# A graph-attention and mixture-of-experts layer on one Trainium2 core: raw tokens in the setup, adjacency in column halves, and another order of the units of a head pair

## The chip, the core and the metric

The kernel runs on one core of a Trainium2 chip. The metric is device time in microseconds (us) of one launch. A core has TensorE (PE, matrix multiplications into PSUM), VectorE (DVE), ScalarE (ACT), GpSimd (POOL) and SyncE (SP, which here only issues DMA transfers). Each engine takes its instructions in the order in which they are written, and a semaphore wait holds everything behind it on that engine.

## What is computed

The layer is graph attention, followed by a mixture of experts that the change doesn't touch:

```python
# N = 2048 tokens, D = 512, H = 16 heads of 32
xn = layernorm(x)                                  # no weights
seq = (xn @ W_seq).reshape(N, H, DH)
s = leaky_relu(score1[:, :, None] + score2[:, None, :], 0.2)   # seq . a1, seq . a2
s = s + (1.0 - adj)[None] * -65500.0
attn = softmax(s, axis=-1)
hidden = einsum('hij,jhd->ihd', attn, seq).reshape(N, D) @ W_out + b_out
x = x + elu(hidden)
x = x + moe_ffn(layernorm(x))
```

## The kernel before

**Units.** The exponential of a leaky ReLU of a sum splits into products of row and column factors, with one of two factor pairs on either side of a threshold. So a head needs, for half of the output rows (IC = 1024), a 0/1 mask of 16 tiles of 128 neighbours by 1024 rows, and matrix products of the mask and of the adjacency with the values. One such product is a unit: 8 row tiles (i), each with 16 matmuls on the mask (L798) and 16 on the adjacency (L802). There are 32 units, four to a pair of heads; the index k in 0..3 of a pair p says head k // 2 and column half k % 2. Masks have MB = 4 buffers, values vs have two (one for each head), sums two.

**The work for a unit.** compare: VectorE compares 6 of the 16 tiles (L653) and ScalarE the other 10 (L600, a steep sigmoid), both against a score row broadcast to all partitions (s1b), which SP loads again (L558) as soon as both have compared. mask_own (L661) and mask_acts (L668) put the adjacency onto VectorE's and ScalarE's tiles; m_ready counts the latter. products (POOL, L742 and L744) scales the values of a head, split_high (ACT, L608) and low_values (DVE, L682) split them into two fp16 parts. TensorE runs the unit when m_ready and sums_ready say so, and lo_ready for a head's first unit. collect (DVE, L675) takes the sums out of PSUM. A unit waits for the collection of the unit two before it. combine (POOL, L752 and L757) scales and adds them into hid. VectorE's loop step (p, k) is: collect(p, k), compare(p + 1, k), low_values if k is odd, mask_own(p + 1, k), mask_acts of the k before.

**The setup.** x is loaded in 4 groups (L185), W_seq on ScalarE's queue (L196), then the constants. VectorE takes mean and variance (stats, L280), GpSimd the inverse root, VectorE normalises x in place (norm, L291). TensorE transposes a tile of x (L429) into PSUM; ScalarE rounds it to a high part (L204), VectorE takes the rest as the low part (low_x, L298). project (L438) is 12 matmuls for a token tile, scores (L449) 12 for four tiles. W_seq is transposed too (L409) for the columns of the scores (L418). Scores go back to token order (L486) and to DRAM as rows (s1_rows). The adjacency comes in 16 loads of 1 MB with three buffers (L193), VectorE turns each into fp8 (L305), TensorE adds up the neighbours of each column (degrees, L460, 64 matmuls), and where there are none VectorE sets all (apply_empty_rows, L395 and L397).

The order is the hand-written order of calls on each engine. The loops of ScalarE, VectorE and GpSimd over the pairs are hardware loops, TensorE's is unrolled.

## Time and profile before

| what | value |
|---|---|
| median of 3 runs | 1078.7 us (1076.36 to 1081.2) |
| the profiled execution itself | 1076.02 us |
| its span, first to last instruction | 1074.2 us |
| TensorE, VectorE, ScalarE, GpSimd busy | 95%, 75%, 60%, 23% of the span |
| granted TensorE clock, mean | 0.981 of full |
| setup, to the first unit | 0 to 129.8 us |
| the 32 units | 129.8 to 505.3 us |
| projection and experts | 505.3 to 1074.2 us |

"Busy" is the time in which an engine had an instruction running. A share over the whole span mixes stages; the setup and the units are to be read apart. In the granted clock 1.00 stands for 2.4 GHz and 0.50 for 1.2 GHz. Names such as arena stand for one large block of SBUF, in which most tiles lie, so a group is best known by its line.

### The profile page before, as it was taken

What the parts mean: (1) busy time and instruction counts of PE and PEld (TensorE: products, weight loads), DVE (VectorE), ACT (ScalarE), POOL (GpSimd) and SP (SyncE); (2) the same over time, 40 slices, a digit from 0 to 9 for tenths busy, and PEclk for the clock granted to TensorE, in tenths of its full rate; (3) what the DMA queues carried; (4) which work ended last, traced back from release to release, by engine and by line L of the source; (5) the groups of instructions that cost most, each with busy time, mean ns of one, the idle gap of its engine ahead of it and who ended that gap; (6) DMA issues with size and microseconds to landing.
All of it is one profiled execution on the core that took longest, in us unless ns stands there. A gap on an engine that the chain in (4) does not pass through costs nothing.

```text
span 1074.2 us, 27252 instructions
## 1 busy us (share of the span) xinstructions
PE 1018.5 (95%) x11304; PEld 894.5 (83%) x11304; DVE 806.5 (75%) x1200; ACT 648.9 (60%) x971; POOL 247.7 (23%) x271
## 2 busy tenths in 40 slices
PE   4799499999999999998999999999999999999998
PEld 4577299999999999998677888888888878878887
DVE  4746999999999999993599633347686569976554
ACT  3226499999999999960456433344345546655441
POOL 1100223333443333344342000000065000006500
PEclk8899699999999999999899999999999999999999
DMA  8357011111111111260834200020044124454242
GB/s 316 118 175 281 20 38 46 42 61 42 62 41 56 47 42 56 83 219 4 298 118 148 108 1 1 1 79 1 1 157 167 59 79 120 132 159 122 79 138 98
DMA packets 51458, 102.45 MB, mean 95 GB/s; under 512 B 5889, under 2 KB 25985, under 8 KB 48770
## 3 DMA queue, kind: packets, MB, share of 16 engines
q1 hardware_dynamic: 44386, 81.68, 22.4%
q10 hardware_dynamic: 3888, 10.72, 2.9%
q0 software_dynamic: 3072, 8.39, 2.4%
q8 instruction: 91, 1.49, 0.6%
q14 instruction: 21, 0.17, 0.0%
HBM read 74.69 MB, written 26.08 MB: 94 GB/s over the span
## 4 chain that ended last, share of the span: by engine, by line
PE 47%; DVE 2%; issue 2%; DMA 1%; POOL 0%; ACT 0%; SPq 0%; POOLq 0%; DVEq 0%; ACTq 0%
PE bank L1177 16%; PE bank L1644 16%; PE bank L1009 3%; PE bank L1721 2%; PE bank L1672 1%; PE bank L1673 1%; PE bank L1675 1%; DMA xs<-sorted_latent_rows 1%; PE bank L1691 1%; PE bank L1665 1%; PE bank L1629 1%; PE bank L1006 1%; PE bank L1627 1%; PE bank L997 1%; PE bank L1018 1%
## 5 line engine op out<-in xcount | busy, mean ns | idle before, releaser
L600 ACT ACTIVATE arena<-arena 128x1024 fp8e4<-128x1024 f32 x320 | 336.4, 1135 | 3.0 <-ACT arena L592 3.0
L798 PE MATMUL bank<-arena 128*128 128x132 f16 x4096 | 283.8, 221 | 15.6 <-DVE arena L682 15.0
L798 PEld LDWEIGHTS bank<-arena 128*128 128x128 fp8e4 x4096 | 245.0, 97 | 17.7 <-DVE arena L682 15.5
L1177 PE MATMUL bank<-xt,up_parts 128*128 128x512 f32 x768 | 186.2, 391 | 0.0
L1644 PE MATMUL bank<-down_parts,h_parts 128*128 128x512 f32 x768 | 184.5, 389 | 0.0
L802 PE MATMUL bank<-arena 128*128 128x66 f16 x4096 | 172.6, 195 | 1.6 <-issue 1.6
L1644 PEld LDWEIGHTS bank<-down_parts,h_parts 128*128 128x128 f32 x768 | 143.9, 188 | 30.2 <-issue 0.2
L653 DVE TENSOR_SCALAR arena<-arena 128x1024 uint8<-128x1024 f32 x192 | 166.4, 933 | 0.0
L1177 PEld LDWEIGHTS bank<-xt,up_parts 128*128 128x128 f32 x768 | 142.3, 188 | 28.7 <-ACT relu_sb L1126 0.2
L802 PEld LDWEIGHTS bank<-arena 128*128 128x128 fp8e4 x4096 | 153.7, 98 | 1.9 <-issue 1.9
L1151 DVE TENSOR_TENSOR relu_sb<-relu_sb 128x512 f32<-128x512 f32 x64 | 44.3, 692 | 117.9 <-ACT relu_sb L1126 117.2
L1126 ACT ACTIVATE relu_sb<-bank 128x512 f32<-128x512 f32 x64 | 38.3, 598 | 148.3 <-PE bank L1177 139.0
L752 POOL TENSOR_TENSOR arena<-arena 128x264 f32<-128x264 f32 x64 | 45.4, 731 | 218.9 <-DVE arena L668 195.9
L668 DVE TENSOR_TENSOR arena<-arena 128x2560 uint32<-128x2560 uint32 x32 | 90.8, 2838 | 0.2
L1145 ACT CAST down_parts<-down_sb 128x512 fp32r<-128x512 f32 x64 | 39.8, 622 | 72.6 <-PE bank L1644 62.9
L1598 POOL DMA_INDIRECT sorted_latent_rows<-latent,slot_idx x32 | 34.7, 1085 | 209.0 <-DVE slot_idx L1464 191.0
L1166 DVE TENSOR_TENSOR down_parts<-down_sb,down_parts 128x512 fp32r<-128x512 f32 x64 | 44.2, 691 | 50.2 <-ACT down_parts L1145 47.4
...
L742 POOL TENSOR_TENSOR arena<-arena 128x512 f32 (+1 forms) x32 | 48.6, 1520 | 63.2 <-ACT arena L209 25.1
L661 DVE TENSOR_TENSOR arena<-arena 128x1536 uint32<-128x1536 uint32 x32 | 56.1, 1753 | 0.6
L675 DVE TENSOR_REDUCE arena<-bank 128x198 f32<-128x396 f32 (+1 forms) x96 | 44.1, 513 | 15.0 <-PE bank L798 15.0
L1009 PE MATMUL bank<-wo_parts,hT 128*128 128x512 f32 x192 | 49.7, 409 | 0.0
...
## 6 DMA issues: line engine op xcount, KB each, us to landing
hid<-in_adjT SPq DMA_DIRECT2D x16, 1024.0 KB, 5.2
arena<-s_rows SPq DMA_DIRECT2D x30, 512.0 KB, 3.7
...
arena<-in_x SPq DMA_DIRECT2D x4, 1024.0 KB, 12.0
...
```

What stands on the lines that cost most here:

```text
L600: last = nc.scalar.activation(m8[:, k, j, :], s1b[:, k % 2, :], ACT.Sigmoid, bias=bias_now[:, k // 2, j:j + 1], scale=STEEP, saturate=False)
L653: last = nc.vector.tensor_scalar(mu8[:, k, j, :], s1b[:, k % 2, :], neg_s2[:, 2 * p + k // 2, j:j + 1], float(ONE8), ALU.is_gt, ALU.mult)
L661: nc.vector.tensor_tensor(mw[:, k, 0:DVE_J, :], mw[:, k, 0:DVE_J, :], adjw[:, 0:DVE_J, cols], ALU.bitwise_and).then_inc(own_masked, 1)
L668: nc.vector.tensor_tensor(mw[:, k, DVE_J:, :], mw[:, k, DVE_J:, :], adjw[:, DVE_J:, cols], ALU.bitwise_and).then_inc(m_ready, 1)
L742: nc.gpsimd.tensor_tensor(vtmp[:, :, c * W1:c * W1 + DH], vh, val[:, :, bass.ds(h, 1)].to_broadcast([P, T, DH]), ALU.mult)
L752: last = nc.gpsimd.tensor_tensor(scaled[:, k % 2, :, c * W1:(c + 1) * W1], sums[:, k % 2, :, c * W1:(c + 1) * W1], coef[:, h, tiles, c:c + ...
L798: last = nc.tensor.matmul(o, m8[:, k, j, i * P:(i + 1) * P], vs[:, b, j, :], start=(j == 0), stop=(j == T - 1))
L802: nc.tensor.matmul(od, adj8[:, ja, (k % 2) * IC + i * P:(k % 2) * IC + (i + 1) * P], vs[:, b, ja, :].rearrange("p (s c) -> p s c", s=2)[:, ...
L1009: last = nc.tensor.matmul(bank[2 + t % 2][:, :], hT[:, t % 2, a, k, :], wo_parts[:, b, k, :], start=False, stop=(n == len(terms) - 1))
L1151: nc.vector.tensor_tensor(r, r, r, ALU.mult).then_inc(sq_ready, 1)
L1177: last = nc.tensor.matmul(bank[6 + s % 2][:, :], sa[:, s % 2, a, k, :], xt[c][:, b, k, :], start=(i == 0), stop=(i == len(mm) - 1))
L1644: last = nc.tensor.matmul(ob[t][:, :], hhl[:, s % 2, a, t * P:(t + 1) * P], sb_[:, s % 2, b, :], start=(n == 0 and (a, b) == TERMS[0]), st ...
```

## The change

W_seq comes transposed, and first on SP's queue. VectorE takes the mean of each of its columns away (centre_w), so that raw tokens can be multiplied by it; x is no longer normalised, and ScalarE multiplies the inverse root in when it copies the projected values out of PSUM (copy_v). Projections use two PSUM banks in turn instead of four. Scores take 8 matmuls instead of 12, with 64 rows out, and their two halves are added after the way back to token order (natural_scores); a second set of 16 transposes makes the rows for DRAM.

The adjacency comes in 32 loads of half a tile row: first the first column half of all 16 tiles, then the second, with five buffers and no wait for x. VectorE casts the even ones, ScalarE the odd ones. Which columns have no neighbour is found from an OR of the 16 tiles (any_neighbour, on VectorE) and 8 matmuls for each half. The second half's come between the first and the second unit.

In a pair, k now says column half k // 2 and head k % 2. The loop body of VectorE has low_values ahead of compare, at k = 2 and 3, and the first collection stands ahead of compare(0, 3).

```diff
-AB = 3
+AB = 5
+HALVES = 2 * T
...
+        SEQ_BANK = [bank[2], bank[3]]
+        WA_BANK = bank[3]
+        ST_BANK = [bank[4], bank[7]]
+        ROW_BANK = [bank[4], bank[7], bank[5], bank[6]]
+        DEG_BANK = [bank[6], bank[7]]
+
+        def cast_source(q):
+            return adj_in[:, q % AB, :], adj8[:, q % T, (q // T) * IC:(q // T + 1) * IC]
...
+            sp.dma_start(wt_sb, w_seqT.rearrange("(c p) k -> p c k", p=P)).then_inc(wt_loaded, 16)
             for g in range(4):
                 sp.dma_start(x_sb[:, 4 * g:4 * g + 4, :],
                              x[512 * g:512 * g + 512, :].rearrange("(t p) d -> p t d", p=P)
                              ).then_inc(x_loaded[g], 16)
-            for g in range(4):
-                sp.wait_ge(x_loaded[g], 16)
-            for n in range(T):
-                if n >= AB:
-                    sp.wait_ge(adj_cast, n - AB + 1)
-                sp.dma_start(adj_in[:, n % AB, :], adjT[n * P:(n + 1) * P, :]).then_inc(adj_loaded[n % AB], 16)
+            for q in range(HALVES):
+                if q >= AB:
+                    sp.wait_ge(cast_by_act if (q - AB) % 2 else cast_by_dve, (q - AB) // 2 + 1)
+                sp.dma_start(adj_in[:, q % AB, :], adjT[(q % T) * P:(q % T + 1) * P, (q // T) * IC:(q // T + 1) * IC]
+                             ).then_inc(adj_loaded[q % AB], 16)
...
-                    nc.scalar.copy(v_sb[:, t, :], SEQ_BANK[t % 4][:, :]).then_inc(v_copied, 1)
+                    act.wait_ge(std_ready, t // 4 + 1)
+                    nc.scalar.activation(v_sb[:, t, :], SEQ_BANK[t % 2][:, :], ACT.Copy,
+                                         scale=rstd[:, t:t + 1]).then_inc(v_copied, 1)
...
+            def cast(*odd):
+                for q in odd:
+                    act.wait_ge(adj_loaded[q % AB], 16 * (q // AB + 1))
+                    src, dst = cast_source(q)
+                    nc.scalar.activation(dst, src, ACT.Copy, scale=-1.0, saturate=False).then_inc(cast_by_act, 1)
...
+            for s in range(8):
+                copy_v(s)
+                if s < 7:
+                    high_x(2 * s + 2, 2 * s + 3)
+                if s % 2:
+                    copy_scores(s // 2)
+                if s >= 2:
+                    cast(2 * s - 3)
+            cast(13)
+            copy_v(8)
+            cast(15)
+            copy_v(9)
+            cast(17)
+            copy_v(10)
+            cast(19)
...
+            def centre_w():
+
+                dve.wait_ge(wt_loaded, 16)
+                for c in range(KD):
+                    last = nc.vector.bn_stats(w_stat6[:, c, :], wt_sb[:, c, :])
+                step(last)
+                for c in range(KD):
+                    last = nc.vector.bn_aggr(w_mv[:, c, :], w_stat6[:, c, :])
+                step(last)
+                for c in range(KD):
+                    last = nc.vector.tensor_scalar(wt_sb[:, c, :], wt_sb[:, c, :], w_mv[:, c, 0:1], None, ALU.subtract)
+                last.then_inc(w_centred, 1)
...
-            def norm(g):
-                dve.wait_ge(std_ready, g + 1)
-                for t in range(4 * g, 4 * g + 4):
-                    nc.vector.tensor_scalar(x_sb[:, t, :], x_sb[:, t, :], mv[:, t, 0:1], rstd[:, t:t + 1],
-                                            ALU.subtract, ALU.mult).then_inc(xn_ready, 1)
...
+            def cast(*even):
+
+                for q in even:
+                    dve.wait_ge(adj_loaded[q % AB], 16 * (q // AB + 1))
+                    src, dst = cast_source(q)
+                    nc.vector.tensor_scalar(dst, src, -1.0, None, ALU.mult, saturate=False).then_inc(cast_by_dve, 1)
...
+            def any_neighbour(half):
+
+                words = slice(half * IC // 4, (half + 1) * IC // 4)
+
+                def cast_up_to(tiles):
+                    dve.wait_ge(cast_by_dve, (T * half + tiles) // 2)
+                    dve.wait_ge(cast_by_act, (T * half + tiles) // 2)
+
+                cast_up_to(8)
+                step(nc.vector.tensor_tensor(anyw, adjw[:, 0:4, words], adjw[:, 4:8, words], ALU.bitwise_or))
+                cast_up_to(12)
+                step(nc.vector.tensor_tensor(anyw, anyw, adjw[:, 8:12, words], ALU.bitwise_or))
+                cast_up_to(16)
+                nc.vector.tensor_tensor(anyw, anyw, adjw[:, 12:16, words], ALU.bitwise_or).then_inc(any_ready, 1)
...
+            def scores_to_tokens():
+                pe.wait_ge(st_copied, 4)
+                for t in range(T):
+                    last = nc.tensor.transpose(bank[5 + t // 8][:, (t % 8) * 4 * H:(t % 8 + 1) * 4 * H],
+                                               sT[:, t * P:(t + 1) * P], ident[0:4 * H, 0:4 * H])
+                last.then_inc(s_in_psum, 1)
+
+            for s in range(8):
+                project(s)
+                if s < 7:
+                    transpose(2 * s + 2, 2 * s + 3)
+                if s % 2:
+                    scores(s // 2)
+            project(8)
+            scores_to_tokens()
+            project(9, 10)
+            scores_to_rows()
+            project(11)
+            degrees(0)
+            project(12, 13, 14, 15)
...
-                    b = k // 2
-                    if k % 2 == 0:
+                    b = k % 2
+                    if k < 2:
+                        act.wait_ge(act_compared, 4 * p + k - 1)
...
-                compare_rows(0, DVE_J, 10)
-                copy_v(10)
-                compare_rows(0, 10, 12)
-                copy_v(11)
-                compare_rows(0, 12, 14)
-                copy_v(12)
-                compare_rows(0, 14, T)
-                copy_v(13, 14, 15)
+                compare_rows(0, DVE_J, DVE_J + 2)
+                copy_v(14)
+                cast(27)
+                compare_rows(0, DVE_J + 2, DVE_J + 4)
+                copy_v(15)
+                cast(29)
+                compare_rows(0, DVE_J + 4, DVE_J + 6)
                 split_high(0, 0)
+                compare_rows(0, DVE_J + 6, T)
+                cast(31)
+                nc.scalar.copy(bias_now[:, 1, :], step_bias[:, 1, :]).then_inc(bias_copied, 1)
+                act.wait_ge(bias_copied, 2)
                 act.wait_ge(s1_staged[1], 16)
-                compare_rows(1, DVE_J, T)
+                compare_rows(1, DVE_J, DVE_J + 4)
                 split_high(0, 1)
+                compare_rows(1, DVE_J + 4, T)
...
+                def body(p, last=False, first=False):
                     for k in range(4):
                         if last and k == 3:
                             split_low()
-                        dve.wait_ge(unit_in_psum, 4 * p + k + 1)
-                        collect(p, k)
+                        if k or not first:
+                            dve.wait_ge(unit_in_psum, 4 * p + k + 1)
+                            collect(p, k)
                         if not last:
+                            if k >= 2:
+                                low_values(p + 1, k % 2)
                             compare(p + 1, k)
-                            if k % 2:
-                                low_values(p + 1, k // 2)
                             mask_own(p + 1, k)
 
                         if k == 0:
@@ -707,29 +778,32 @@
...
-                scale_columns()
-                cast_adjacency(10)
                 dve.wait_ge(seq_in_psum, 8)
                 compare(0, 0)
-                cast_adjacency(11, 12, 13, 14, 15)
-                apply_empty_rows((0, 1))
+                cast(24, 26)
                 mask_own(0, 0)
+                cast(28)
+                low_values(0, 0)
                 mask_acts(0, 0)
-                apply_empty_rows((2, 3))
+                cast(30)
                 dve.wait_ge(seq_in_psum, T)
                 compare(0, 1)
-                low_values(0, 0)
                 mask_own(0, 1)
+                any_neighbour(1)
+                low_values(0, 1)
                 mask_acts(0, 1)
-                low_values(0, 1)
+                apply_empty_rows((2, 3))
                 compare(0, 2)
                 mask_own(0, 2)
+                mask_acts(0, 2)
+                dve.wait_ge(unit_in_psum, 1)
+                collect(0, 0)
                 compare(0, 3)
                 mask_own(0, 3)
-                mask_acts(0, 2)
-                with dve.Fori(0, PAIRS - 1) as p:
-                    body(p, False)
-                body(PAIRS - 1, True)
+                body(0, first=True)
+                with dve.Fori(1, PAIRS - 1) as p:
+                    body(p)
+                body(PAIRS - 1, last=True)
...
-                        b = k // 2
-                        if k % 2 == 0:
+                        b = k % 2
+                        if p == 0 and k == 1:
+                            degrees(1)
+                        if k < 2:
                             pe.wait_ge(lo_ready, 2 * p + b + 1)
```

Three places of the order of instructions follow. The first is the start of VectorE's queue. Before, the constants and then x are waited for:

```order
L309 MEMSET score_columns 128x352
L312 TENSOR_SCALAR arena<-arena 128x4x16 [waits consts_loaded]
L312 TENSOR_SCALAR arena<-arena 128x4x16
L280 BN_STATS arena<-arena 128x6 [waits x_loaded0]
L280 BN_STATS arena<-arena 128x6 x3
```

Now the same start, with the weights in front:

```order
L348 MEMSET score_columns 128x512
L351 TENSOR_SCALAR arena<-arena 128x4x16 [waits consts_loaded]
L351 TENSOR_SCALAR arena<-arena 128x4x16
L306 BN_STATS arena<-arena 128x6 [waits wt_loaded]
L306 BN_STATS arena<-arena 128x6 x3
L309 BN_AGGR arena<-arena 128x2 [waits dve_step]
L309 BN_AGGR arena<-arena 128x2 x3
L312 TENSOR_SCALAR arena<-arena 128x512 [waits dve_step]
L312 TENSOR_SCALAR arena<-arena 128x512 x3
```

Nine instructions on the weights' columns moved ahead of the statistics of x, and TensorE's first instruction waits for them.

The second place is VectorE between the mask of the first unit and the first collection. Before, from mask_acts(0, 0) on (L395 and L397 are the empty columns, L653 a comparison, L661 and L668 the masks, L682 low_values):

```order
L395 TENSOR_SCALAR arena<-bank 128x512
L397 TENSOR_TENSOR arena<-arena 128x16x128
L653 TENSOR_SCALAR arena<-arena 128x1024 x6
L682 TENSOR_TENSOR arena<-arena 128x16x66
L661 TENSOR_TENSOR arena<-arena 128x1536
L668 TENSOR_TENSOR arena<-arena 128x2560
L682 TENSOR_TENSOR arena<-arena 128x16x66
L653 TENSOR_SCALAR arena<-arena 128x1024 x6
L661 TENSOR_TENSOR arena<-arena 128x1536
L653 TENSOR_SCALAR arena<-arena 128x1024 x6
L661 TENSOR_TENSOR arena<-arena 128x1536
L668 TENSOR_TENSOR arena<-arena 128x2560
```

Now, from the comparison for the second unit (L723) on, with any_neighbour at L409 to L413, low_values at L752 and the collection at L745:

```order
L731 TENSOR_TENSOR arena<-arena 128x1536 [waits dve_compared]
L409 TENSOR_TENSOR hid<-arena 128x1024 [waits cast_by_act,cast_by_dve]
L411 TENSOR_TENSOR hid<-hid,arena 128x1024 [waits cast_by_act,cast_by_dve,dve_step]
L413 TENSOR_TENSOR hid<-hid,arena 128x1024 [waits cast_by_act,cast_by_dve,dve_step]
L752 TENSOR_TENSOR arena<-arena 128x16x66 [waits hi_copied]
L738 TENSOR_TENSOR arena<-arena 128x2560 [waits own_masked,act_compared]
L420 TENSOR_SCALAR arena<-bank 128x512 [waits deg_in_psum]
L422 TENSOR_TENSOR arena<-arena 128x16x128 [waits dve_step]
L420 TENSOR_SCALAR arena<-bank 128x512 [waits deg_in_psum,dve_step]
L422 TENSOR_TENSOR arena<-arena 128x16x128 [waits dve_step]
L723 TENSOR_SCALAR arena<-arena 128x1024 [waits s1_staged_lo,dve_step]
```

The OR, the second half's empty columns and one wait for TensorE stand there now between the second unit's comparison and the third's.

The third place is a step with k odd in the loop on VectorE. Before:

```order
L675 TENSOR_REDUCE arena<-bank 128x132
L653 TENSOR_SCALAR arena<-arena 128x1024 [waits s1_staged_hi]
L653 TENSOR_SCALAR arena<-arena 128x1024 x5
L681 REGISTER_ALU
L682 TENSOR_TENSOR arena<-arena 128x16x66 [waits hi_copied]
L660 REGISTER_ALU
L661 TENSOR_TENSOR arena<-arena 128x1536 [waits dve_compared]
L668 TENSOR_TENSOR arena<-arena 128x2560 [waits own_masked,act_compared]
```

Now, the step with k = 3:

```order
L745 TENSOR_REDUCE arena<-bank 128x198 x2
L745 TENSOR_REDUCE arena<-bank 128x132
L752 TENSOR_TENSOR arena<-arena 128x16x66
L723 TENSOR_SCALAR arena<-arena 128x1024 x6
L731 TENSOR_TENSOR arena<-arena 128x1536
L738 TENSOR_TENSOR arena<-arena 128x2560
```

low_values moved from behind the comparison to the place right behind the collection.

## Rows read from the trace of the kernel before

**Rows 1.** Stretches: engines busy and count, TensorE clock, DMA share, GB/s; loop of units.
```profile
164.80:480.90 316.10, 313.92 (x6933) 311.99 (x6931) 314.56 (x312) 302.15 (x302) 114.61 (x135) 1.00 0.20 67
```

**Rows 2.** VectorE in order of time, one pair of loop steps: start us, us, instruction.
```profile
350.86 1.38 DVE L675 TENSOR_REDUCE arena<-bank 128x198 f32<-128x396 f32 x3
352.15 4.62 DVE L653 TENSOR_SCALAR arena<-arena 128x1024 uint8<-128x1024 f32 x6
356.70 1.25 DVE L682 TENSOR_TENSOR arena<-arena 128x1056 f16<-128x1056 f32 x1
357.87 1.75 DVE L661 TENSOR_TENSOR arena<-arena 128x1536 uint32<-128x1536 uint32 x1
359.53 2.81 DVE L668 TENSOR_TENSOR arena<-arena 128x2560 uint32<-128x2560 uint32 x1
...
363.57 6.09 DVE L653 TENSOR_SCALAR arena<-arena 128x1024 uint8<-128x1024 f32 x6
...
374.11 1.38 DVE L675 TENSOR_REDUCE arena<-bank 128x198 f32<-128x396 f32 x3
```

**Rows 3.** TensorE in order of time, two tiles of one unit.
```profile
345.39 1.09 PE L798 MATMUL bank<-arena 128*128 128x132 f16 x16
...
346.83 1.09 PE L798 MATMUL bank<-arena 128*128 128x132 f16 x16
```

**Rows 4.** Who waited for whom, 128 to 500 us: us in total, times, longest.
```profile
PEld bank L798 <- DVE arena L675: 2.2, 9, 0.3
```

**Rows 5.** VectorE in order of time, setup, and the second collection of the loop.
```profile
12.68 2.46 DVE L280 BATCH_NORM_STATS2 arena<-arena 128x6 f32<-128x512 f32 x4
...
20.88 1.91 DVE L291 TENSOR_SCALAR arena<-arena 128x512 f32<-128x512 f32 x4
...
88.05 4.06 DVE L653 TENSOR_SCALAR arena<-arena 128x1024 uint8<-128x1024 f32 x6
...
108.46 2.29 DVE L397 TENSOR_TENSOR arena<-arena 128x2048 uint32<-128x2048 uint32 x1
...
163.52 1.38 DVE L675 TENSOR_REDUCE arena<-bank 128x198 f32<-128x396 f32 x3
```

**Rows 6.** TensorE in order of time, the setup up to the first unit.
```profile
12.37 3.54 PE L409 MATMUL bank<-arena,hid 128*128 128x128 f32 x16 [12.37 <-DMA arena<-in_a_mask]
16.68 4.85 PE L418 MATMUL bank<-arena 128*128 128x32 f32 x32 [0.77 <-ACT arena L215]
...
25.68 0.78 PE L438 MATMUL bank<-w_high,x_high 128*128 128x512 f32 x1
...
30.18 0.39 PE L438 MATMUL bank<-w_high,x_high 128*128 128x512 f32 x1
...
57.69 1.03 PE L429 MATMUL bank<-arena 128*128 128x128 f32 x8
...
78.85 0.50 PE L438 MATMUL bank<-w_high,x_high 128*128 128x512 f32 x1
...
95.33 4.49 PE L460 MATMUL bank<-arena 128*128 128x512 fp8e4 x20
...
129.83 0.29 PE L798 MATMUL bank<-arena 128*128 128x132 f16 x1 [15.01 <-DVE arena L682]
```

**Rows 7.** A stretch as in rows 1, in which adjacency loads land.
```profile
20.00:26.50 6.50, 5.86 (x26) 5.17 (x26) 4.84 (x8) 2.46 (x5) 1.92 (x1) 0.50 1.00 423
```

**Rows 8.** DMA issues by line: KB each, median us to landing.
```profile
hid<-in_adjT SPq DMA_DIRECT2D x16, 1024.0 KB, 5.2
arena<-s_rows SPq DMA_DIRECT2D x30, 512.0 KB, 3.7
```

**Rows 9.** ScalarE in order of time, first comparisons.
```profile
87.31 4.27 ACT L600 ACTIVATE arena<-arena 128x1024 fp8e4<-128x1024 f32 x4
```

**Rows 10.** GpSimd in order of time, same stretch as rows 2.
```profile
364.78 1.52 POOL L742 TENSOR_TENSOR arena<-arena 128x512 f32 x1
...
374.40 1.24 POOL L752 TENSOR_TENSOR arena<-arena 128x264 f32<-128x264 f32 x2 [5.33 <-DVE arena L668]
```

322 lines of the change are left out of this document (153 added, 169 removed).

## The prediction, made before the changed kernel ran

> **What bounds the kernel now.** I read the stretches first, then the engines in order of time, and stage by stage, since the mean over the span hides that two stages have different limits. In the 32 units TensorE looks like the limit, but between 164.8 and 480.9 us VectorE is busy for 314.6 of 316.1 us, with no gap to give away [rows 1]. A pair of its loop steps takes 23.25 us, from 350.86 to 374.11 [rows 2]. A tile of a unit takes 1.44 us on TensorE [rows 3], so two units of eight tiles take 23.04. The two are within 1%, VectorE is the slower one, and TensorE waits a little for its collections, nine times by this view [rows 4]. So it matters little when the first unit starts; what counts is the time at which VectorE ends collect(0, 1) and with it frees the fourth unit. I call that time W. It is 164.8 now: 163.52 and three reductions [rows 5]. From W to the end of the last unit, 505.3, it is 340.5 us, and from there to the end of the span 568.9, which the change doesn't touch. In the setup nothing is saturated: TensorE starts at 12.4, waits for the low parts of x, and stands still for 15.0 us ahead of the first unit at 129.83, with VectorE's queue in front of it [rows 6].
>
> **The start.** VectorE must now centre the weights before TensorE does anything: 2.46 us of statistics as for four x tiles, four passes of 512 columns like the norms, 1.91, and 0.5 for small ones [rows 5], 4.9 in all. In return the 1 MB of weights and the constants are no longer behind 2 to 3 MB of other loads. With 423 GB/s [rows 7] that megabyte takes 2.5 us after the first bytes; I take 6.2 us for the end of this wait, which puts the first matmul at 11.3. The bound above is that the constants land at 12.3 as before [rows 6]; this costs 6 at the start and, as statistics then run while TensorE works, 4 at W.
>
> **Projections.** On TensorE then follow the transposes of W 3.5, two of x at half clock 1.9, the score columns 4.85 and one projection 4.5 (25.68 to 30.18), so 26.2 [rows 6]. Up to the scores in token order: 8 projections at 2.75 (six from 78.85 to 95.33), 14 tiles transposed at 0.5 (eight instructions in 1.03, four to a tile), 32 score matmuls at 0.23 instead of 48, and 1.4 for the way to tokens [rows 6]: 22.0 + 7.2 + 7.4 + 1.4 = 38, so 64.2, where it is 78.9 now. This holds if TensorE never waits. For each projection step of 4.65 us ScalarE has a copy of values, two high parts, a cast and half a score copy, about 3.0; VectorE has 1.9, and 4.9 in the three steps with statistics. The two PSUM banks cover that: a projection waits for the copy two before. The norms (16 passes, 7.7 us of VectorE) and their wait for GpSimd are gone; what is late next is the low part of x, with 1 to 3 us to spare.
>
> **To the first unit.** Two projections and the transposes into rows end at 71.5. Four small copies, the transfer to DRAM and the one back, 3.7 each [rows 8], exponentials, one copy and one cast put the score rows into SBUF at 82.5. The adjacency does not hold this up: with five half loads in flight at 1.3 us each (0.52 MB at 423 GB/s) the sixteenth half is cast at 64.5. From 83.6 on ScalarE's own queue is the path: a table load 1.3, ten comparisons at 1.05 [rows 9], two value copies 1.1, casts 27 and 29 at 1.05 each, the split 1.0, waits 0.4, which gives 100.0; with mask_acts, 2.8 [rows 2], the first unit starts at 102.8. TensorE ends its projections at 87.0 and stands still for 16, as now.
>
> **From the first unit to W**, all on VectorE: cast 0.6, comparison 4.0 [rows 5], own mask 1.7, the OR 3.4 (three times 1024 words, where 1536 take 1.75), low values 1.2, mask 2.8 [rows 2]: 116.5. It waits for the 8 degree matmuls behind the first unit (11.5 us, and an estimated 3.3 for a start at half clock, where everything takes twice as long) until 118.6; behind this wait stand the third and fourth masks. Then 6.1 for two column blocks of empty columns (2.29 and the flags [rows 5]), 4.0, 1.7, 2.8 and a collection 1.3: the third unit at 134.5, TensorE having waited 3. Then 4.5, 1.7, 5.5, 1.7, 2.8, 1.3, and W is 151.9. The same sum over the old order of calls gives 163.1 where the row says 164.8; I add that 1.7, so W = 153.6, 11.2 earlier. The first unit gains 25 of which 14 are lost again, because the second half's casts, OR and empty columns moved from ahead of it to behind it.
>
> **From W to the end.** The work in a loop step is the same. What shifts is the company of VectorE's comparison. With GpSimd's products beside it (from 364.78) it takes 6.09, with a combine (from 374.40) about 4.6 [rows 2, 10], alone 4.06 [rows 5]. At k = 2 and 3 the combine now falls beside the collection and low_values, and I estimate 0.35 + 0.45 saved in four steps, 5.6 over seven passes. TensorE's own pace limits this: 29 units at 11.52 are 334.1, 1.6 for gaps in its instruction stream, and 1.4 as the sixth unit now waits for low_values: W + 337.1. If nothing is saved it is W + 340.5. I take 338. In the trace the split (a wait of VectorE for ScalarE would be new, as low_values moved forward by 4.6) is done 4 us ahead of VectorE's step, so I cost this at nothing; if that lead were gone, 1 to 2 us a time.
>
> The combine beside two-input operations is where the Trainium skill speaks against me. The row shows a comparison slowed in the company of GpSimd [rows 2, 10]. By the Trainium skill (SBUF — State Buffer, Who interferes with whom) a VectorE instruction with two SBUF inputs contends with a GpSimd one that reads SBUF, and one of the two blocks fully, while a reduction never does. By that rule only the part beside the collection is saved, and the sum would be nearer to W + 340.
>
> **The sum.** 505.3 becomes 153.6 + 338 = 491.6, which is 13.7 less. The profiled execution took 1076.0 (span 1074.2 and 1.8 around it), so 1062.3 for its like; it stands 2.7 under the median of 1078.7. On the median: **1065.0**.
>
> **Rivals.** (A) VectorE remains the limit and nothing is saved by the shift: W + 341.7 with the low_values wait, 495.3, a gain of 10: 1068.7. For it: VectorE's 99.5% [rows 1]. Together with late constants (4) it is 1072.7. (B) The first unit decides, as TensorE's 95% would have it: 25.3 gained, 1053.4. Against it: the same row, and TensorE's waits for collections [rows 1, 4]. (C) The early gain isn't there at all, because ScalarE, with 16 casts more, holds the projections: then the scores are in token order near 75, not 64, and W falls by 0 to 3: 1076 to 1079. Against it: 3.0 of 4.65 us a step. (D) Slower: half loads land no faster than whole ones. A load now lands in 5.2 us, and a half-size one from DRAM in 3.7, not 2.6 [rows 8], so some of the time doesn't shrink. With 2.7 us a half the path above waits for loads 15 to 31, W is 168.7 and the end 506.7 to 510.4 (1080 to 1084); with 3.0 W is 175.5, the end 513.5 to 517.2, and the kernel takes 1087 to 1090. It loses from 2.5 us a half on, and measurably from 2.8. Against it: 423 GB/s with only three loads in flight [rows 7].
>
> The Trainium skill sides with D in part: DMA: Bandwidth & Descriptors, Rules for kernel authors, wants transfers of at least 1 MiB for full bandwidth, and these are half of that. The row shows 423 GB/s for whole ones and nothing for halves.
>
> **How the numbers follow.** The forecast (gain 11 to 17) 0.55, A with or without late constants 0.2, B 0.03, C 0.12, D 0.06, the rest 0.04. What a measurement of this kernel can tell from no change is about 0.5%, 5.4 us. Faster by more than that holds the forecast, B and most of A: 0.78; within it C and a little of A: 0.15; slower D and the rest: 0.07. The range: below, W 151.9 and TensorE's pace give 489.0, a gain of 16.3, and runs go 2.3 under their median, 1059; above, C's better end, 1076.
>
> **What would show it.** Right: first matmul near 11, scores in token order near 66, first unit near 104 with ScalarE the last one waited for, a gap of about 3 us on TensorE ahead of the third and again the fourth unit, collect(0, 1) ending near 154, and comparisons at k = 2 and 3 shorter than 6.1 and 4.6. Wrong: VectorE waiting for loads in the setup, TensorE waiting for x's low parts by more than 3 us in total, VectorE waiting for hi_copied in the loop, or W to the end over 342.

## The result and the profile after

The changed kernel takes 1065.5 us (median of 4 runs, 1063.7 to 1066.7), the kernel before 1078.2 beside it: a ratio of 0.987, 95% interval 0.986 to 0.989. That is faster by 1.3%, small but with the whole interval below 1, and 0.5 us from the forecast.

The profiled execution took 1063.7 us. I read it by marks. T is the start of the transposes that bring the scores into token order (their end stands in this table, as in the prediction), U the start of the first unit, W the end of the second collection, L the start of the last collection, which is the end of the last unit.

| | before | predicted | after |
|---|---|---|---|
| scores in token order (end) | 78.9 | 64.2 | 63.0 |
| U | 129.8 | 102.8 | 104.2 |
| W | 164.8 | 153.6 | 150.5 |
| L | 505.3 | 491.6 | 491.5 |
| W to L | 340.5 | 338.0 | 341.0 |
| L to the end of the span | 568.9 | 568.9 | 570.4 |

TensorE in order of time (start us, us, instruction, idle before and what ended it); these answer [rows 6]:

```profile
13.71 3.65 PE L468 MATMUL bank<-arena 128*128 128x128 f32 x16 [13.71 <-DVE arena L312]
...
26.45 1.03 PE L487 MATMUL bank<-arena 128*128 128x128 f32 x8
...
53.57 1.03 PE L487 MATMUL bank<-arena 128*128 128x128 f32 x8
...
61.80 1.21 PE L517 MATMUL bank<-arena 64*128 64x64 f32 x16
...
104.17 0.27 PE L874 MATMUL bank<-arena 128*128 128x132 f16 x1 [18.33 <-DVE arena L738]
...
134.24 0.29 PE L874 MATMUL bank<-arena 128*128 128x132 f16 x1 [3.90 <-DVE arena L745]
...
150.63 0.23 PE L874 MATMUL bank<-arena 128*128 128x132 f16 x1 [3.16 <-DVE arena L745]
```

The first matmul waits for the centred weights (L312) until 13.7, later than before. From there to T it never stands: three double steps of projections take 9.04 us each. Then it stands 18.3 us for the first mask, 3.9 for the first collection and 3.2 for the second.

VectorE over the same time, answering [rows 5]:

```profile
8.65 0.42 DVE L351 TENSOR_SCALAR arena<-arena 128x64 f32<-128x64 f32 x2 [7.25 <-DMA arena<-in_a_mask]
...
62.13 0.69 DVE L345 TENSOR_SCALAR arena<-hid 128x1024 fp8e4<-128x1024 f32 x1 [4.67 <-DMA hid<-in_adjT]
...
97.03 1.26 DVE L752 TENSOR_TENSOR arena<-arena 128x1056 f16<-128x1056 f32 x1 [7.42 <-ACT arena L673]
101.20 2.82 DVE L738 TENSOR_TENSOR arena<-arena 128x2560 uint32<-128x2560 uint32 x1 [2.91 <-ACT arena L665]
...
140.69 4.06 DVE L723 TENSOR_SCALAR arena<-arena 128x1024 uint8<-128x1024 f32 x6
...
149.19 1.38 DVE L745 TENSOR_REDUCE arena<-bank 128x198 f32<-128x396 f32 x3
```

ScalarE is the last one waited for ahead of the first unit, twice, 7.4 us for the split (L673) and 2.9 for the comparisons (L665). From 101.2 to W VectorE has no wait left.

The loop, VectorE, then GpSimd beside it, answering [rows 2, 10]:

```profile
347.07 1.38 DVE L745 TENSOR_REDUCE arena<-bank 128x198 f32<-128x396 f32 x3
348.37 1.34 DVE L752 TENSOR_TENSOR arena<-arena 128x1056 f16<-128x1056 f32 x1
349.64 6.08 DVE L723 TENSOR_SCALAR arena<-arena 128x1024 uint8<-128x1024 f32 x6
...
361.46 1.32 DVE L752 TENSOR_TENSOR arena<-arena 128x1056 f16<-128x1056 f32 x1
362.71 4.45 DVE L723 TENSOR_SCALAR arena<-arena 128x1024 uint8<-128x1024 f32 x6
...
372.90 6.30 DVE L723 TENSOR_SCALAR arena<-arena 128x1024 uint8<-128x1024 f32 x6
...
384.94 4.63 DVE L723 TENSOR_SCALAR arena<-arena 128x1024 uint8<-128x1024 f32 x6
...
394.02 1.38 DVE L745 TENSOR_REDUCE arena<-bank 128x198 f32<-128x396 f32 x3
```

```profile
360.43 1.24 POOL L826 TENSOR_TENSOR arena<-arena 128x264 f32<-128x264 f32 x2 [5.96 <-DVE arena L738]
361.85 1.44 POOL L831 TENSOR_TENSOR hid<-arena 128x264 f32 x1 [0.18 <-POOL arena L826]
...
385.50 0.87 POOL L831 TENSOR_TENSOR hid<-arena 128x264 f32 x1 [0.19 <-POOL arena L826]
```

Four steps take 46.95 us, from 347.07 to 394.02; two pairs of steps as in [rows 2] took 46.56 (350.86 to 397.42). The comparisons are as long as before. The last addition of a combine takes 1.44 us beside low_values (361.85) where it takes 0.87 beside a comparison (385.50). These two rows also show how long the addition stays beside the comparison: it ends 0.6 us into the one at k = 3 and 1.4 us into the one at k = 1.

The stretch of the loop, answering [rows 1], who TensorE waited for, answering [rows 4], and the loads, answering [rows 8]:

```profile
150.49:466.66 316.17, 312.04 (x6878) 311.03 (x6879) 315.25 (x309) 292.65 (x292) 122.43 (x135) 0.99 0.19 66
```

```profile
PE bank L874 <- DVE arena L752: 3.3, 5, 0.7
```

```profile
hid<-in_adjT SPq DMA_DIRECT2D x32, 512.0 KB, 5.7
arena<-s_rows ACTq DMA_DIRECT2D x2, 512.0 KB, 4.7
```

VectorE is busy for 315.3 of 316.2 us. A half load lands in 5.7 us with up to five in flight. From 66 to 72 us, where the DMA engines were busy throughout, they moved 371, 416 and 395 GB/s in stretches of 2 us, which is 1.3 to 1.4 us a half, as the prediction had it. ScalarE still waits for a load at a costly place, right ahead of the table load and the comparisons of mask 0:

```profile
84.29 1.06 ACT L224 ACTIVATE arena<-hid 128x1024 fp8e4<-128x1024 f32 x1 [3.15 <-DMA hid<-in_adjT]
```

The table load then starts at 85.36.

### The profile page after: what moved, and what is told of

It is laid out like the page before. It is cut to its first block, busy times and chain, and to the rows that moved or that the text cites. A ratio compares the mean times of both kernels' runs of the same rounds, so it can differ in the third digit from the quotient of the medians.

```text
span 1061.9 us, 27192 instructions
## 1 busy us (share of the span) xinstructions
PE 1003.7 (95%) x11256; PEld 889.3 (84%) x11256; DVE 801.6 (75%) x1197; ACT 666.4 (63%) x990; POOL 247.5 (23%) x271
## 4 chain that ended last, share of the span: by engine, by line
PE 48%; issue 2%; DVE 2%; DMA 1%; POOL 0%; ACT 0%; SPq 0%; POOLq 0%; DVEq 0%; ACTq 0%
PE bank L1253 16%; PE bank L1720 16%; PE bank L1085 3%; PE bank L1797 2%; PE bank L1748 1%; PE bank L1749 1%; PE bank L1751 1%; DMA xs<-sorted_latent_rows 1%; PE bank L1767 1%; PE bank L1705 1%; PE bank L1741 1%; PE bank L1082 1%; PE bank L1703 1%; PE bank L1073 1%; PE bank L1094 1%
## 5 line engine op out<-in xcount | busy, mean ns | idle before, releaser
L665 ACT ACTIVATE arena<-arena 128x1024 fp8e4<-128x1024 f32 x320 | 336.4, 1135 | 2.5 <-ACT arena L657 1.4
L874 PE MATMUL bank<-arena 128*128 128x132 f16 x4096 | 285.1, 221 | 29.4 <-DVE arena L738 18.3
L723 DVE TENSOR_SCALAR arena<-arena 128x1024 uint8<-128x1024 f32 x192 | 166.2, 932 | 0.0
L878 PEld LDWEIGHTS bank<-arena 128*128 128x128 fp8e4 x4096 | 154.3, 98 | 0.1
L1686 POOL DMA_INDIRECT y_gathered<-sorted_expert_rows,slot_idx x32 | 32.6, 1018 | 153.6 <-DMA sorted_expert_rows<-expert_y 132.8
L745 DVE TENSOR_REDUCE arena<-bank 128x198 f32<-128x396 f32 (+1 forms) x96 | 44.2, 516 | 14.2 <-PE bank L874 14.2
## 6 DMA issues: line engine op xcount, KB each, us to landing
sorted_latent_rows<-zeros SPq DMA_DIRECT2D x1, 4992.0 KB, 18.3
```

The source lines that it names most:

```text
L665: last = nc.scalar.activation(m8[:, k, j, :], s1b[:, k % 2, :], ACT.Sigmoid, bias=bias_now[:, k % 2, j:j + 1], scale=STEEP, saturate=False)
L723: last = nc.vector.tensor_scalar(mu8[:, k, j, :], s1b[:, k % 2, :], neg_s2[:, 2 * p + k % 2, j:j + 1], float(ONE8), ALU.is_gt, ALU.mult)
L745: last = nc.vector.reduce_sum(sums[:, k % 2, t0:t0 + n, :], bank[3 * (k % 2) + g][:, 0:n * WV].rearrange("p (t s c) -> p t c s", t=n, s=2) ...
L874: last = nc.tensor.matmul(o, m8[:, k, j, i * P:(i + 1) * P], vs[:, b, j, :], start=(j == 0), stop=(j == T - 1))
L878: nc.tensor.matmul(od, adj8[:, ja, (k // 2) * IC + i * P:(k // 2) * IC + (i + 1) * P], vs[:, b, ja, :].rearrange("p (s c) -> p s c", s=2)[ ...
```

## What the runs were to settle

Theory T: all of VectorE's work from the first unit to W, and its pace in the loop, set the end; when the first unit starts does not. Rival R1: the first unit, or TensorE's pace after it, decides. (The letters of theories and rivals have nothing to do with the marks T, U, W and L.) Three more questions came from the terms that missed: why nothing was saved in the loop, what ScalarE's queue is worth, and which part of the change brought the gain at W.

Single executions of one kernel differ by up to 12 us ("norms back": 1067.7 to 1079.9), so I read the marks in each trace beside the medians. A trace is of one execution, so a mark of one trace carries that execution's scatter. The change itself was run once more beside three of the later kernels.

> The changed kernel itself, unchanged, on the chip of the next three kernels, so that differences of two or three microseconds can be read against it. Every theory: 1065.5 us, and in the trace W (the end of the second collection) 46.3 us behind the first unit's start and the end of the last unit 341.0 us behind W.

The table holds all the kernels. In the eight traces whose loop is untouched W to L is 341.0 to 341.4, so a difference of one microsecond there can be read.

| kernel | T | U | W | W to L | L to end | median | ratio to before |
|---|---|---|---|---|---|---|---|
| the change | 61.8 | 104.2 | 150.5 | 341.0 | 570.4 | 1065.5 | 0.987 (0.986 to 0.989) |
| the change again | 63.8 | 107.9 | 154.3 | 341.1 | 571.0 | 1066.7 | 0.987 (0.984 to 0.989) |
| 5 us more on VectorE | 59.7 | 101.5 | 153.8 | 341.1 | 570.8 | 1073.9 | 0.995 (0.993 to 0.997) |
| late first unit | 62.8 | 119.8 | 152.2 | 341.1 | 578.3 | 1065.8 | 0.987 (0.985 to 0.989) |
| low parts behind | 62.1 | 105.2 | 152.9 | 342.7 | 572.2 | 1069.9 | 0.991 (0.988 to 0.994) |
| last casts on VectorE | 62.5 | 104.9 | 151.7 | 341.2 | 573.6 | 1065.4 | 0.985 (0.982 to 0.988) |
| values first | 59.6 | 100.2 | 147.8 | 341.0 | 571.8 | 1065.1 | 0.986 (0.983 to 0.988) |
| low parts mixed | 62.4 | 103.1 | 150.4 | 341.9 | 571.0 | 1065.1 | 0.985 (0.982 to 0.987) |
| no multiplications on GpSimd | 62.6 | 105.9 | 153.7 | 336.0 | 570.5 | 1060.8 | 0.982 (0.979 to 0.984) |
| a row to ScalarE | 63.3 | 106.1 | 152.9 | 338.4 | 573.2 | 1063.1 | 0.985 (0.983 to 0.988) |
| norms back | 69.4 | 111.2 | 157.8 | 341.4 | 572.2 | 1073.2 | 0.995 (0.992 to 0.997) |
| quarter loads | 62.8 | 107.7 | 154.8 | 341.3 | 569.5 | 1066.3 | 0.990 (0.987 to 0.993) |
| score rows before loads | 60.1 | 100.7 | 147.5 | 338.6 | 572.5 | 1061.0 | 0.983 (0.982 to 0.985) |

Read it by the columns. Leaving out "norms back", T still goes from 59.6 to 63.8, and L to the end from 569.5 to 578.3. The second is scatter in the mixture of experts that nothing here touches. The first goes with TensorE's granted clock in the first projection, as the last section shows.

## Does the first unit decide?

**Five microseconds more on VectorE**, ahead of the comparison of mask 3:

```
 collect(0, 0)
+for _ in range(3):
+    words of mw[:, 3, 0:6] = adjw & adjw; wait for them
 compare(0, 3)
```

> Three needless operations of 1.68 us each on VectorE (words of the adjacency joined with themselves into the mask buffer that the next comparison overwrites, each waited for before the next) stand between the collection of the first unit and the comparison of mask 3: 5.0 us plus three short drains, 5.2 us in all. The result is untouched. Theory T (the stretch up to the second collection and the unit loop are VectorE's, so that all of VectorE's work ahead of the loop is on the path): +5.2 us against the changed kernel, 1070.7. Rival R1 (the start of the first unit decides, and TensorE's pace after it): nothing before the fourth unit is touched, TensorE pays at most what exceeds its own slack there, +0 to +1.5 us, 1065.5 to 1067.

**Late first unit:**

```
-if p == 0 and k == 1:
-    degrees(1)
+if p == 0 and k == 0:
+    degrees(1)
+    pe.wait_ge(m_ready, 2)
```

> TensorE is made to wait with the first unit until the mask of the second is ready too, and counts the neighbours of the second column half before it instead of behind it. The first unit then starts near 118.0 instead of 104.2, 13.8 us later; no work is added. Theory T: VectorE never waits for a unit there (it comes to the first collection at 132.8 and to the second at 149.2, the units would end near 130.8 and 142.4), so W, the end of the second collection, stays at 150.5 and the time at 1065.5, +0 to +1 us. Rival R1 (the first unit decides): TensorE's three waits ahead of the second to the fourth unit, 1.3, 3.9 and 3.2 us, can take up 8 of the 13.8 us, the rest is paid: +5.5 us or more, 1071.

TensorE and VectorE of the second kernel in order of time:

```profile
115.99 3.35 PE L535 MATMUL bank<-hid,arena 128*128 128x512 fp8e4 x8 [29.10 <-DVE hid L413]
119.80 0.23 PE L875 MATMUL bank<-arena 128*128 128x132 f16 x1 [0.47 <-DVE arena L738]
```

```profile
150.86 1.38 DVE L745 TENSOR_REDUCE arena<-bank 128x198 f32<-128x396 f32 x3
```

The first unit starts at 119.8, T + 57.0 instead of T + 42.4, and VectorE still waits for nothing: W is T + 89.3 against T + 88.7 and T + 90.5 in the two traces of the change. The median is 1065.8. A first unit that stands 12.9 to 14.6 us further behind T costs nothing that can be measured; R1 falls. In the first kernel U to W grows from 46.3 to 52.3 us, 6.0 for 5.2 added, and W to L stays at 341.1, so that added work is paid in full. Its median rose by more, 7 to 8 us, from times that scatter over 10 us: 5.2 us on the ratio of the change would be 0.992, just below the interval. What the trace doesn't hold of that I leave open.

## The low parts and the company of GpSimd

**Low parts behind the comparison again:**

```
-if k >= 2:
-    low_values(p + 1, k % 2)
 compare(p + 1, k)
+if k >= 2:
+    low_values(p + 1, k % 2)
 mask_own(p + 1, k)
```

> In the unit loop the low parts of the values are taken behind the comparison again (steps k = 2 and 3), instead of between collection and comparison. Theory T has two halves. In the loop, the semaphore that VectorE waits for between comparison and own mask is hidden again behind the low parts: 46.95 us in four steps go back to about 46.55, 7 times 0.4 is 2.8 us less. At the end, the last pair's second unit waits for its low values, which come a comparison (4.5 us) and a drain later, and three units of 11.5 us follow them: +5.6 us. Net +2.8 us, 1068.3. Rival R2 (the loop's pace alone decides, the tail is covered): -2.8 us, 1062.7. Rival R3 (the combination's company beside the comparison costs VectorE what the prediction charged, 0.8 us in four steps): +5.6 from the loop, +8 or more with the tail, 1073.

```profile
168.81 0.29 PE L874 MATMUL bank<-arena 128*128 128x132 f16 x1 [4.04 <-DVE arena L752]
```

```profile
440.28 1.38 DVE L745 TENSOR_REDUCE arena<-bank 128x198 f32<-128x396 f32 x3
...
459.10 1.69 DVE L752 TENSOR_TENSOR arena<-arena 128x1056 f16<-128x1056 f32 x1
...
495.61 1.39 DVE L745 TENSOR_REDUCE arena<-bank 128x198 f32<-128x396 f32 x3 [6.31 <-PE bank L874]
```

From the second collection to the 27th (149.19 to 440.96 in the change, 151.64 to 440.28 here) VectorE needs 288.6 us instead of 291.8: 3.1 less, where 2.8 were expected. The end takes back 4.8, where 5.6 were expected, and W to L is 1.7 longer. R2 and R3 fall by W to L; the median, 1069.9, is 1.6 us above the forecast and its times go from 1063.7 to 1075.0. But TensorE also waits 4.0 us once for low parts, after the fourth unit, and then hardly again. That led to the next kernel.

**Low parts mixed**, behind for the first six pairs, ahead for the last, on top of "values first" below:

```
-with dve.Fori(1, PAIRS - 1) as p:
+with dve.Fori(1, PAIRS - 2) as p:      # low parts behind
     body(p)
+body(PAIRS - 2, ahead=True)
```

> As the kernel before it, and in the unit loop the low parts of the values come behind the comparison for the first six pairs and ahead of it only for the last, where the tail waits for them. Theory T: the run with the low parts behind everywhere took four steps in 46.56 us for 46.95 and lost 4.1 us at the end; this keeps the first, 6 times 0.4 is 2.4 us, and not the second: 1058.1, W to end 338.6. Rival R2' (the gain in the loop was bought by the later end, VectorE being held by TensorE's chain): W to end stays at 341.0, 1060.5.

W to L is 341.9. The saving of VectorE is there and the last low parts come in time, yet nothing is gained: R2' holds. TensorE stands 4.0 us for low parts at 166.25 and from there to 492.3 needs 326.1 us for 28 units, of which 322.6 is its own pace. The change loses the same 4 us in five waits of 0.5 to 0.7 us and 0.7 in its instruction stream, the other order in one piece. From there on TensorE is nearly at its own pace, so VectorE's saving has nothing left to shorten.

**No multiplications on GpSimd:**

```
-scaled = sums * coef        # two instructions
-hid = scaled[0:W1] + scaled[W1:]
+hid = sums[0:W1] + sums[W1:]
```

> GpSimd's two multiplications in the combination of every unit are left out (it only adds the two halves of the sums, so the output is not the reference's); GpSimd then works 1.24 us less beside each step of VectorE. Theory P (GpSimd's company costs VectorE in proportion to how long it lasts, about 0.45 us for each microsecond beside a comparison): the comparisons of steps 1 and 3 fall from 4.63 and 4.45 us to about 4.1, those of 0 and 2 by 0.4 to 0.5 us each, four steps take 45.2 us of VectorE's work, so that TensorE's 46.08 us become the pace: W to end 341.0 - 7.3 times 0.87, about 334.7, time 1059. Rival Q (a comparison pays a lump for being near GpSimd's work, whatever its length, or pays for the products alone): less than 0.5 us in four steps, W to end 338 or more, time 1062.5 to 1065.5.

VectorE in order of time:

```profile
340.83 1.38 DVE L745 TENSOR_REDUCE arena<-bank 128x198 f32<-128x396 f32 x3
...
343.29 5.71 DVE L723 TENSOR_SCALAR arena<-arena 128x1024 uint8<-128x1024 f32 x6
...
355.91 4.07 DVE L723 TENSOR_SCALAR arena<-arena 128x1024 uint8<-128x1024 f32 x6
...
365.72 5.54 DVE L723 TENSOR_SCALAR arena<-arena 128x1024 uint8<-128x1024 f32 x6
...
377.00 4.06 DVE L723 TENSOR_SCALAR arena<-arena 128x1024 uint8<-128x1024 f32 x6
...
385.51 1.38 DVE L745 TENSOR_REDUCE arena<-bank 128x198 f32<-128x396 f32 x3
```

The comparisons without GpSimd beside them fall to 4.07 and 4.06, as long as alone, and the other two by 0.4 and 0.8. Four steps take 44.68 us and TensorE is the pace: W to L 336.0. Q's numbers are out (it wanted W to L 338 or more), and P's are the nearer ones (334.7). But P's reason, a price in proportion to time, is not shown. In this kernel the addition ends before the comparisons of k = 1 and 3 start, so they have no company left; and in the change 0.6 us of an addition beside a comparison cost 0.39 us (4.45 for 4.06) where 1.4 us of a combine cost 0.57. 336.0 is also the measured end of TensorE's own pace: the prediction's lower bound was W + 337.1.

**A row to ScalarE.** The same gain with the work done: on top of "values first", ScalarE takes one comparison more in step k = 0 of every pair but the first.

```
+def rows_of(p, k): return 5 if k == 0 and p != 0 else 6
-for j in range(DVE_J):                   # VectorE
+for j in range(rows_of(p, k)):
-compare_rows(k, DVE_J, T)                # ScalarE
+compare_rows(k, rows_of(p, k), T)
```

> The kernel with the values first and, in the unit loop, one of VectorE's six comparisons of step k = 0 on ScalarE (five rows of 16 left on VectorE in that step, six in the others). Theory B (in the loop VectorE's 46.95 us for four steps are the pace and TensorE's 46.08 only just below it, ScalarE at 44.4 with 2.5 us of waiting has room for one row more): VectorE loses a comparison in GpSimd's company, 1.05 us, and comes to 45.9; ScalarE comes to 45.4; TensorE sets the pace, 46.08, and no longer waits for low values: W to end 336.5 to 337 instead of 341.0, as in the kernel without GpSimd's multiplications (336.0). With the setup of that kernel 1060.8. Rival S (ScalarE has no room: its splits wait for GpSimd's products, which wait for VectorE): W to end 341 or more, 1065 or more.

```profile
372.98 5.64 DVE L733 TENSOR_SCALAR arena<-arena 128x1024 uint8<-128x1024 f32 x5
...
393.43 1.38 DVE L757 TENSOR_REDUCE arena<-bank 128x198 f32<-128x396 f32 x3
```

```profile
354.64 1.07 ACT L686 CAST arena<-arena 128x1056 f16<-128x1056 f32 x1 [0.87 <-POOL arena L830]
```

Five comparisons take 5.64 us where six took 6.30. I had counted 1.05 for the one taken away, its share of a slowed comparison; it is 0.66, close to the price of one alone (4.06 for six). That GpSimd's work beside it doesn't become less would explain it; no run separates that. Four steps take 46.29 us (347.14 to 393.43) and W to L 338.4, between B and S and nearer to B. ScalarE's wait for GpSimd shrinks from 2.5 to 0.9 us, less than the 1.05 of a row, so there is hardly room for a second one. The median, 1063.1, is 2 us under that of "values first", but the intervals of the two ratios overlap almost wholly: the gain is read from W to L.

## What ScalarE's queue is worth

**Last casts on VectorE:** casts 25, 27, 29 and 31.

```
-cast(24, 26)                             # VectorE; likewise 28, 30
+cast(24, 25, 26, 27)
```

> The casts 25, 27, 29 and 31 of the half loads go from ScalarE to VectorE. On VectorE each takes 0.69 us and three of them fall into its waits of 7.4 and 2.9 us ahead of the first unit; on ScalarE four of 1.05 us and a wait of 3.15 us for a load go. Theory T: ScalarE's queue is what the first unit and VectorE's own work up to W wait for, so the first unit starts 5 to 6 us sooner (near 98.5), W falls by 4.3 to 5.5 us to near 145.5, and the time is 1060.5. Rival R4 (the loads, or the values of the last tokens, decide the first unit, not ScalarE's queue): the first unit within 2 us of 104.2, VectorE 2.8 us fuller, +0 to +2 us, 1066. Rival R1 would give the same as T here.

**Values first**, with the casts moved:

```
 copy_v(13)
+copy_v(14); copy_v(15)
+nc.scalar.activation(warm, bias_now[:, 0, 0:1], ACT.Sigmoid)
 act.wait_ge(s1_staged[0], 16)
 compare_rows(0, DVE_J, DVE_J + 2)
-copy_v(14)                               # and copy_v(15) further down
```

> Casts 25, 27, 29 and 31 on VectorE as before, and ScalarE's queue in another order: it scales the values of tokens 14 and 15 before its comparisons of mask 0 instead of between them, and loads the table of the comparisons with one needless element while it would wait for the score rows. With the casts alone moved, the first unit stayed at 104.9, since GpSimd's products waited for the last values until 91.9 (then took 4.7 us) and ScalarE stood 2.75 us for them. Theory T (ScalarE's queue, now its order rather than its length, is last at the first unit, and VectorE's work is the rest up to W): the values are there near 85.5, the products near 90, ten comparisons of 1.04 us and one split of 1.06 us from 85.2 end at 96.7, the first unit starts at 99.5, 5 us sooner, W near 145.5, the time 1060.5. Rival R4 (the landing of the score rows or of the last loads decides the first unit): first unit within 2 us of 104, time 1065.

GpSimd's first product and VectorE's mask beside it, in the kernel with the casts moved alone:

```profile
92.01 2.83 POOL L821 TENSOR_TENSOR arena<-arena 128x512 f32<-128x512 f32 x1 [24.89 <-ACT arena L225]
```

```profile
91.56 1.75 DVE L736 TENSOR_TENSOR arena<-arena 128x1536 uint32<-128x1536 uint32 x1
```

I expected 5 to 6 us of the first and got none: U is T + 42.4 as in the change. With the casts gone ScalarE stood 3.2 us for the score rows and began its comparisons at 85.1, T + 22.6, only 1.0 us sooner than in the change (T + 23.6); then it stood 2.75 us for GpSimd, whose product was issued behind the last values (91.9) and took 2.83 instead of 1.07. The second brings U to T + 40.7, and W to T + 88.2 from 88.7 and 90.5: 0.5 to 2.3 us instead of 5. Its ratio (0.986) can't be told from that of the change. T's 1060.5 was wrong twice: I priced ScalarE's queue and not what it would wait for next. R4's 1065 is what came out both times. In the first kernel its reason holds in part (score rows and last values). In the second it does not: VectorE waits 1.6 us for the score rows, but ScalarE, the last one, waits for TensorE's last projection and from there to U for nothing:

```profile
83.65 0.69 ACT L226 ACTIVATE arena<-bank,arena 128x512 f32<-128x512 f32 x1 [2.03 <-PE bank L508]
```

**Norms back:**

```
+def norm(g):
+    dve.wait_ge(std_ready, g + 1)
+    for t in range(4 * g, 4 * g + 4):
+        x_sb[:, t, :] = (x_sb[:, t, :] - mv[:, t, 0:1]) * 1.0
-pe.wait_ge(x_loaded[t // 4], 16)
+pe.wait_ge(xn_ready, t + 1)
```

> Raw tokens are undone in their cost: a pass of VectorE over every token tile (the mean taken away, which the centred weights make needless) between the statistics with GpSimd's inverse root and the transposes on TensorE, 16 passes of 0.48 us, with the wait for the root. Theory T (of VectorE's queue only its head, up to the first projection, holds TensorE; later steps have room, VectorE 1.9 of 4.65 us): the first x transpose about 1 us later, the low parts of the weights 3 us later, scores in token order and W about 3 us later than now, 1068.5. Rival N (the passes and their wait were what made the projections slow before the change): 7.7 us or more at the scores in token order and at W, 1073 or more; of 14 us gained, more than half.

```profile
18.30 1.97 PE L497 MATMUL bank<-arena 128*128 128x128 f32 x8 [0.99 <-DVE arena L336]
...
32.01 1.25 PE L497 MATMUL bank<-arena 128*128 128x128 f32 x8
...
46.47 1.23 PE L497 MATMUL bank<-arena 128*128 128x128 f32 x8 [1.43 <-DVE x_low L343]
```

T is 69.4, 7.6 and 5.6 later than in the two traces of the change; U is T + 41.8 and W T + 88.4, so both move along, W by 7.3 and 3.5, and the median by 6 to 8 us. Rival N is nearer and my theory for this run falls: VectorE's queue holds TensorE not at its head alone, the second pair of transposes starts 5.6 us later (32.01 for 26.45) and the rest comes step by step. This trace ran at a granted clock of 1.00 from 20 to 26.5 us and the change at 0.74 and 0.64; against the three traces at 1.00 there (T 59.6 to 60.1) T is 9.3 to 9.8 later. The passes and their wait are thus some 4 to 10 of the 14.3 us gained at W (10.5 in the second trace). What remains belongs to the column halves, the order of units and the fewer score matmuls together; I did not separate those.

**Quarter loads:**

```
-sp.dma_start(adj_in[:, b, :], adjT[rows, half])
+for c in range(2):
+    sp.dma_start(adj_in[:, b, half of it], adjT[rows, quarter])
```

> Every load of half a block of adjacency rows (512 KB) is issued as two of 256 KB, with the same buffers and the same order. Theory T (the loads have room: five in flight, VectorE and ScalarE's waits for them of 4.7 and 3.2 us lie beside other waits): first unit and W within 1 us, 1065.5 to 1066.5. Rival D' (the size of a load sets its rate, as the prediction's case D had it for halves): the loads land 0.5 us or more later each, loads 15 to 31 hold the casts, and W and the time rise by 5 us or more, 1070.5.

```profile
hid<-in_adjT SPq DMA_DIRECT2D x64, 256.0 KB, 4.4
```

W is T + 92.0, 1.5 to 3.3 later than in the change, and the ratio 0.990 for 0.987; the intervals overlap, so the runs don't show a loss and only the trace suggests one. A quarter lands in 4.4 us where a half takes 5.7, so the time doesn't shrink with the size, but the 5 us of D' are out. For halves the case D of the prediction, 2.5 us a half or more, is out too: the stretches above give 1.3 to 1.4.

**Score rows before loads**, on top of "a row to ScalarE":

```
 for q in range(HALVES):
+    if q == 23:
+        sp.wait_ge(s1_staged[0], 16); sp.wait_ge(s1_staged[1], 16)
```

> The kernel with a row of comparisons on ScalarE, and SyncE issues the half loads 23 to 31 only when both score rows have landed; cast 23 goes to VectorE with the others. In the traces so far the two broadcasts of score rows (512 KB each) landed in 4.6 to 4.7 us in three kernels and in 7.3 to 8.3 us in the other seven, with up to five half loads beside them, and VectorE and ScalarE then stood 2 to 5 us for them. Theory L (the half loads take the bandwidth of the rows): the rows land in 4.7 us or less, the first unit starts 39 to 41 us behind the scores in token order for 42.8 in the kernel before it, W follows by 2 to 3 us, and the times scatter less: 1060.5. Rival M (the landing of the rows is set by the rows' own way, to DRAM and back, whatever else is in flight): 7 to 8 us again, and the later loads then hold casts 24 to 31: first unit the same or 1 to 3 us later, 1063 to 1066.

Issues by line in this kernel, and in the order of time TensorE's first unit:

```profile
arena<-s_rows ACTq DMA_DIRECT2D x2, 512.0 KB, 4.2
s_rows<-arena ACTq DMA_DIRECT2D x1, 128.0 KB, 3.8
```

```profile
100.71 0.27 PE L888 MATMUL bank<-arena 128*128 128x132 f16 x1 [16.61 <-DVE arena L752]
```

The rows land in 4.2 us, for 7.9 in the kernel it is built on and 7.7 in the second trace of the change. M falls. U is T + 40.7 for T + 42.8, W T + 87.4 for T + 89.6, as L forecast, but one trace each doesn't show that the rows did it. Over the twelve traces before this one the rows landed in 4.6 to 4.8 us in four and in 7.3 to 8.3 in eight, so a quick landing comes without the edit too. And U is T + 40.7 as well in "values first" (rows in 7.9) and in "low parts mixed" (4.6): in these three ScalarE takes the last values at T + 24.1, right behind TensorE, and in "a row to ScalarE" 2 us later. So the slow landing cost nothing in "values first"; what cost 2 us in "a row to ScalarE" is not separated.

The median is 1061.0, five runs between 1060.3 and 1062.6, all of them under the nine of the change (1063.7 to 1068.1). By the ratios it is 0.4% under the change: its interval (0.982 to 0.985) lies just under that of the first measurement (0.986 to 0.989) and overlaps that of the second (0.984 to 0.989). From "a row to ScalarE" (0.983 to 0.988) the ratios can't tell it.

## The prediction, step by step

**The start** was mis-sized. The constants land at 8.65 and not at 6.2, and the first matmul starts at 13.7, not 11.3 (the terms 6.2 and 4.9 add up to 11.1; the 4.9 came out at 5.1). The 2.4 lost there were made up again: the first projection ends 12.7 us behind the first matmul, where my sum had 14.9, and a double step takes 9.04 for 9.3, so the scores came 1.2 ahead of the forecast. That TensorE never waits for x's low parts was right.

**The first unit** was near (102.8 forecast, 104.2 measured), with ScalarE last as forecast, but the number flatters the sum: the scores were 1.2 early and the rest 2.6 too short. ScalarE's queue was sized rightly, 15.8 us for 16.4. It started at 85.4 instead of 83.6, because cast 25 stood 3.15 us for its load, a wait that the sum put at nothing. In other traces the score rows, which share the time with half loads (4.6 to 8.3 us to land), come later than that: in the order of the change U is T + 41.8 to 42.4 where they land in 4.6 to 4.8 us (three traces), and T + 43.2 to 44.9 where they take 7.3 or more (four traces).

**W** was 3.1 too late. Two terms: the adjustment of 1.7, taken from the difference between my sum and the old row, did not carry over (the sum without it gives 151.9), and compare(1, 0) has no company, 4.06 at 140.69 where I put 5.5. The wait for the degree matmuls, 2.1 in the sum, did not occur: VectorE came there 1.5 later than forecast, at 118.0, and went on at once, which took up the late first unit. The TensorE waits ahead of the third and fourth unit, 3.9 and 3.2, were forecast as about 3.

**W to the end** was 3.0 too short, and here the step failed and not its size. I took 0.8 us off four steps because the combine moves beside the collection and low_values. The comparisons are unchanged: 21.46 in four steps (6.08, 4.45, 6.30, 4.63), where two pairs of steps before had 4.62, 6.09, 4.49 and 6.29, 21.49 in all. The move itself happened: the addition that ended 1.3 us into a comparison before (376.69, in one that began at 375.40) ends 0.6 us into it now (363.29, begun at 362.71). It could not end sooner because low_values reads two inputs, and beside it the addition takes 1.44 for 0.87. The kernel before, VectorE and GpSimd:

```profile
375.40 4.49 DVE L653 TENSOR_SCALAR arena<-arena 128x1024 uint8<-128x1024 f32 x6
...
375.82 0.87 POOL L757 TENSOR_TENSOR hid<-arena 128x264 f32 x1 [0.18 <-POOL arena L752]
```

What failed is the price: I let a comparison's cost shrink with the time that GpSimd stays beside it, and it stayed at 4.45 for 4.49. Why the shorter overlap costs as much is open. "No multiplications on GpSimd" shows only that without any overlap these comparisons take 4.06. The four steps even became 0.4 longer, about half of it because low_values no longer hides the drain between comparison and own mask, and half because low_values itself takes 1.34 and 1.32 beside GpSimd where it took 1.25. The sentence on the Trainium skill (SBUF — State Buffer, Who interferes with whom) had warned of a part of that; its W + 340 is nearer to 341.0 than mine. Rival A named 341.7 and was right for this term.

The two misses, -3.1 and +3.0, cancel in the sum: 491.5 for 491.6. That the forecast of 1065.0 is better than its parts is luck. The range's lower end was also set 1 us too low: a gain of 16.3 and 2.3 under the median give 1060.1, not 1059. Of the signs, "comparisons at k = 2 and 3 shorter than 6.1 and 4.6" came out at 6.08 and 4.45, of which only the second counts; "VectorE waiting for loads in the setup" did occur (4.7 us at 62.13), but ended 0.2 us before the scores it would have waited for anyway.

**Rivals.** B fell: delaying the first unit by 13 to 15 us changes nothing. C fell: TensorE has no wait in the projections. D fell with 1.3 to 1.4 us a half, though a load did hold ScalarE once, as said above, and by the quarter loads the rule of the Trainium skill (DMA: Bandwidth & Descriptors, Rules for kernel authors) for at least 1 MiB doesn't decide here: at a quarter of that size the trace shows 1.5 to 3.3 us lost at W, and the times none that is clear.
